# Loading the adjacency of a two-layer graph attention kernel through GpSimd's DMA queue, converted to bfloat16 on the way

## The chip, the cores and the metric

The kernel runs on one core of one Trainium2 chip. A core has a matrix engine (PE in the profile, with its weight loads listed as PEld), a vector engine (DVE), a scalar engine (ACT), GpSimd (POOL) and a sync engine (SP) that mostly issues transfers; 16 DMA engines move the data. The metric is the device time of one execution in microseconds (us). Every version has to give the outputs of the reference.

## The reference, cut to what matters

```python
# x: (8192, 128) float32; adj: (8192, 8192) int32 of zeros and ones, one in 1024 is a one
h = jnp.maximum(_layernorm(x), 0.0)
Whs, Wht, Whc = h @ Ws, h @ Wt, h @ Wc            # 64, 64 and 128 wide
z = jnp.where(adj > 0, Whs @ Wht.T, -9e15)
x = x + softmax(z, axis=-1) @ Whc                 # layer 0
h = jnp.maximum(_layernorm(x), 0.0)
Wh = h @ W
e = leaky_relu((Wh @ a1)[:, None] + (Wh @ a2)[None, :], 0.2)
x = x + elu(softmax(jnp.where(adj > 0, e, -9e15), axis=1) @ Wh)   # layer 1
```

The adjacency is 256 MB. Everything else is small: x is 4 MB.

## The kernel before

The 8192 queries are cut into 64 tiles of 128. For a tile, a key matters only if one of its 128 queries has an edge to it. The kernel therefore reads the adjacency of the tile (4 MB), finds the keys that are used, gathers at most 32 of every block of 128 keys with one-hot matrix products, and computes attention over these 2048 slots alone. The one-hot matrices and the gathered mask of each tile are stored to HBM (`sel_pick`, `sel`), and layer 1 works from them, so the adjacency is read only once, in layer 0. If a block had more than 32 used keys, a branch that works over all keys would be taken; with these inputs it is not.

The input `adjB` is laid out so that a tile is four chunks (c = 0 to 3) of 1 MB, in each of which a partition gets one contiguous row of 2048 int32 (16 key blocks of 128 queries). A chunk lands in `adj_st[:, c]`, of which there is one buffer for each c, named `arena` in the profile like most buffers here.

The stages of a run, by the profile's time: a preparation of about 75 us (layer norm of x in four quarters, transposes, projections), in which GpSimd's `make_h` (line 598) normalises two of every four rows of tiles; the tile sweep over 64 tiles up to about 940 us, which is a software pipeline that works on tile i's adjacency while it computes scores of tile i-2 and sums of tile i-4; a second preparation; and layer 1 from about 1000 us to the end.

In the sweep, step i (`tile_step`) holds on each engine, in program order:

- DVE: `convert` of chunks 0, 1 and 2 (line 1465: int32 to an fp8 mask, plus or minus one half), between them `maximum` (1512, 1515) and `make_pick` (1490, the one-hot matrices), then `indicate` (1472, which keys are used), `finish` (1529), and two `part_maximum` (1499) over the scores.
- ACT: evacuations from PSUM (1112, 1118, 1125), and among them `convert` of chunk 3 (line 1141), right ahead of the first of two `exps` (1132), which PE's first scores product of the next tile (764) waits for.
- PE: the gathers (725, 737, 752), the scores (763, 764, 769), the weighted sums (790).
- SP: `tile_io`. First the four `load_chunk` of the next tile, then the stores of the one-hot matrices (`store_pick`, line 454) and of the mask (`store_mask`, 448), 256 KB each, then one store of 64 KB (442) and one load of 64 KB (437).

`load_chunk(t, c)` waits until the previous tile's chunk in the same buffer has been converted (`conv_done` counts DVE's three, `conv_act` ACT's one) and then issues one transfer of 1 MB (line 434). SP is in order, so a chunk that waits for its buffer holds back what stands behind it: chunk 3 stands behind chunk 2, and the stores stand behind both. GpSimd does nothing in the sweep.

Of the kernel before, what the change touches and what calls it, by code (L numbers as in the profile page):

```python
# [11 lines left out]
BF16 = mybir.dt.bfloat16  # L12
F8 = mybir.dt.float8e4
I32 = mybir.dt.int32
# [4 lines left out]
P = 128  # L19
# [29 lines left out]
def gnn_kernel(nc, x, xB, adj, adjB, Ws, Wt, Wc, W1, a1, out, x_mid, sel, sel_pick):  # L49
    N = x.shape[0]  # L50
    TILES = N // P
# [10 lines left out]
    with ExitStack() as ctx:  # L62
# [6 lines left out]
        def sem(name):  # L69
            return ctx.enter_context(nc.semaphore(name))  # L70
# [3 lines left out]
        def part(start, words, dt=F32):  # L74
            view = arena[:, start:start + words]
            return view if dt == F32 else view.bitcast(dt)


        ADJ, VALS, KP, QQ, MASK, CC, POSX, VS, PT, K2, MS, END, TOP = (
            0, 8192, 16384, 20480, 28672, 32768, 34816, 36864, 40992, 43040, 44064, 45088, 46080)  # L80
        adj_st = part(ADJ, 8192, I32).rearrange("p (c b n) -> p c b n", c=4, n=P)
        c_vals = part(VALS, 8192, F16).rearrange("p (b v) -> p b v", v=2 * D)
        kp = part(KP, 4096, F16).rearrange("p (b k) -> p b k", k=2 * NHID)
        cq_hi = part(QQ, 4096, F16)
# [174 lines left out]
        adj_in = [sem(f"adj_in{c}") for c in range(4)]  # L259
        conv_done = sem("conv_done")  # L260
        conv_act = sem("conv_act")
# [71 lines left out]
        PREP = TILES // 4  # L333
# [4 lines left out]
        def wait(eng, s, value):  # L338
            if not (isinstance(value, int) and value <= 0):
                eng.wait_ge(s, value)  # L340

        def within(t, lo, hi):

            return not isinstance(t, int) or lo <= t < hi
# [12 lines left out]
        def there(i, d):  # L357

            return within(i, d, TILES + d)
# [36 lines left out]
        def by_choice(eng, selected_keys, all_keys):  # L396

            eng.wait_ge(decided, 1)
            ok = eng.value_load(edge_ok[0:1, 0:1], min_val=0, max_val=1)
            with eng.If(ok != 0):  # L400
                selected_keys()
            eng.wait_ge(decided_redo, 1)
            again = eng.value_load(redo[0:1, 0:1], min_val=0, max_val=1)
            with eng.If(again != 0):
                all_keys()
# [5 lines left out]
        def _(sp):  # L411
            def load_rows(src, mode, quarters=range(4)):
                n = TILES // 4
                for q in quarters:
                    rows = slice(q * n, (q + 1) * n)
                    sp.dma_start(x_all[mode][:, rows, :], src[:, rows, :]).then_inc(xall_in[q], 16)
# [7 lines left out]
                with nc.allow_non_contiguous_dma(reason="256 numbers"):  # L424
                    sp.dma_start(a_sb[:, :], a1.rearrange("(k d) o -> d (k o)", k=2)).then_inc(w_in, 16)

            def load_chunk(t, c):

                if c < 3:
                    wait(sp, conv_done, t * 3 + (c - 2))  # L430
                else:
                    wait(sp, conv_act, t)
                rows = adjB[bass.ds(t, 1), c, :, :, :].rearrange("o p b n -> p (o b) n")
                sp.dma_start(adj_st[:, c, :, :], rows).then_inc(adj_in[c], 16)  # L434

            def load_x(t, b):
                sp.dma_start(x_t[:, b, :], x[bass.ts(t, P), :]).then_inc(x_in[b], 16)

            def store_y(t, b):

                sp.wait_ge(y_ready, t + 1)
                sp.dma_start(x_midB[:, bass.ds(t, 1), :].rearrange("p o d -> p (o d)"), y_t[:, b, :]
                             ).then_inc(y_out[b], 16)

            def store_mask(t, b):

                sp.wait_ge(m_evac, t * 2 + 2)
                sp.dma_start(sel[bass.ds(t, 1), :, :].rearrange("o p n -> p (o n)"),
                             m_sel[:, b, :, :].rearrange("p s w -> p (s w)")).then_inc(m_out[b], 16)

            def store_pick(t, b):

                sp.wait_ge(pick_ready, t + 1)
                sp.dma_start(sel_pick[bass.ds(t, 1), :, :].rearrange("o p n -> p (o n)"), pick_w[:, b, :]
                             ).then_inc(pick_out[b], 16)

            def tile_io(i, b):
                if within(i, 0, TILES - 1):
                    for c in range(4):
                        load_chunk(i + 1, c)  # L460
                if there(i, 1):
                    store_pick(i - 1, 1 - b)
                if there(i, 2):
                    store_mask(i - 2, b)
                if there(i, 4):
                    store_y(i - 4, b)
                if within(i, 4, TILES + 2):
                    load_x(i - 2, b)
                if isinstance(i, int) and i == TILES:
                    sp.wait_ge(conv_done, TILES * 3)  # L470
                    sp.wait_ge(conv_act, TILES)
                    sp.wait_ge(y_out[0], 16 * (3 * TILES // 8))
                    sp.wait_ge(y_out[1], 16 * (3 * TILES // 8))
                    load_rows(x_midB, 1, range(3))
                if isinstance(i, int) and i == 4:
                    sp.wait_ge(mean_ready, 1)
                    sp.dma_start(w_sb[:, 0, :], W1).then_inc(w_in, 16)
# [1 line left out]
            load_rows(xB, 0, (0,))  # L479
            load_weights()  # L480
            load_rows(xB, 0, (1, 2, 3))
            for c in range(4):
                load_chunk(0, c)
            load_x(0, 0)
            load_x(1, 1)
            tile_sweep(sp, tile_io, fetched=False)
            sp.wait_ge(y_out[0], 16 * (TILES // 2))
            sp.wait_ge(y_out[1], 16 * (TILES // 2))
# [86 lines left out]
        @block.gpsimd  # L575
        def _(pool):
            nc.gpsimd.memset(ident[:, :], 0.0).then_inc(ident0, 1)
            pool.wait_ge(ident0, 1)
            nc.gpsimd.affine_select(out=ident[:, :], in_=ident[:, :], compare_op=ALU.not_equal, fill=1.0,
                                    base=0, pattern=[[-1, P]], channel_multiplier=1).then_inc(ident_ready, 1)  # L580
            nc.gpsimd.memset(tri_f[:, :], 1.0).then_inc(tri0, 1)
            pool.wait_ge(tri0, 1)
            nc.gpsimd.affine_select(out=tri_f[:, :], in_=tri_f[:, :], compare_op=ALU.is_ge, fill=0.0,
                                    base=0, pattern=[[1, P]], channel_multiplier=-1).then_inc(const_pool, 1)
            nc.gpsimd.iota(slot_i[:, :], pattern=[[1, SLOT]], base=1, channel_multiplier=0).then_inc(const_pool, 1)
            nc.gpsimd.memset(ones_b[:, :], 1.0).then_inc(const_pool, 1)
            nc.gpsimd.memset(bounds[:, :], 0.0).then_inc(const_pool, 1)

            def make_h(G, b, mode):

                tiles = range(G * NGRP + 2, G * NGRP + NGRP)
                for k, (lo, hi) in enumerate(SPANS[mode]):
                    if lo <= tiles[0] < hi:
                        pool.wait_ge(rstd_ready, BEFORE[mode] + k + 1)
                pool.wait_ge(xall_in[G // 4], 16 * (mode + 1))
                wait(pool, hT_ps_ready, mode * PREP + G - 1)
                for i, tile in enumerate(tiles):
                    last = nc.gpsimd.tensor_scalar(h_sb[mode][:, b, (2 + i) * P:(3 + i) * P], x_all[mode][:, tile, :],
                                                   rstd[:, 2, tile:tile + 1], rstd[:, 3, tile:tile + 1],
                                                   ALU.mult, ALU.add)  # L600
                last.then_inc(h_pool, 1)

            for mode in range(2):
                for G in range(PREP):
                    make_h(G, G % 2, mode)

            def mask(tau, m):

                pool.wait_ge(g_adj_in[m // 2], 16 * (tau + 1))
                wait(pool, masked, tau * STEPS + (m - 3))  # L610
                pool.sem_inc(pool_settled, 1)
                nc.gpsimd.tensor_scalar(off_sb[:, m % 4, :], adj_sb[:, m // 2, CW:2 * CW], 0.0, OFF,
                                        ALU.is_le, ALU.mult).then_inc(mask_pool, 1)

            def masks(layer):
                for m in range(1, STEPS, 2):
                    mask(layer * TILES, m)
                with pool.Fori(1, TILES) as t:
                    for m in range(1, STEPS, 2):
                        mask(t + layer * TILES, m)  # L620

            def all_keys():
                masks(0)
                masks(1)

            by_choice(pool, lambda: None, all_keys)
# [1365 lines left out]
```

## Time and profile before

| | |
|---|---|
| Runs | 1398.08, 1403.41 and 1406.76 us; median 1403.41 |
| Profiled execution, its own span | 1402.6 us |
| Busy in it: PE / DVE / ACT / POOL | 1276.6 / 1250.6 / 1024.8 / 32.3 us |
| HBM read / written | 319.03 / 41.94 MB |
| Adjacency loads | 256 of 1024 KB, median 7.3 us from issue to landing |

The profile is of one execution. A line names the source line, the engine, the operation, and what is written from what; a median or mean is per instruction. "[1.13 <-DMA ...]" behind an instruction says that its engine sat idle for 1.13 us and what ended that. The chain of waits follows the end of the work back, at each step to what released it. "DMA share" is the mean busy share of the 16 DMA engines.

### The profile page before, as it was taken

The numbers are of one execution on the slowest core, as the hardware profiler recorded it, in microseconds if no ns is written. First come the engines' busy times: TensorE is split into PE (matmuls) and PEld (weight loads), VectorE is DVE, ScalarE is ACT, GpSimd is POOL, SyncE is SP. The second block draws the span as 40 slices with busy tenths as digits, with TensorE's granted clock in tenths as the row PEclk, the third lists the DMA queues.
The fourth block names the chain that finished last, engine by engine and source line by source line (L and its number), as shares of the span: only waits on it lengthen the run. The fifth ranks groups of instructions, "written<-read, shape, count | busy, mean of one in ns | idle before, by whom it ended". The sixth has DMA issues, their size and how long they took to land.

```text
span 1402.6 us, 76097 instructions
## 1 busy us (share of the span) xinstructions
PE 1276.6 (91%) x31819; PEld 1131.9 (81%) x31947; DVE 1250.6 (89%) x2323; ACT 1024.8 (73%) x2036; POOL 32.3 (2%) x75
## 2 busy tenths in 40 slices
PE   5867899999999999999999999989899999999996
PEld 3656788888888888878878888877799999999995
DVE  8877799999999999989999999847899999999996
ACT  5755576767667677667676666748789999999994
POOL 2200000000000000000000000013000000000000
PEclk9979899999999999999999999999899999999998
DMA  6678899999999999999999999531134244334322
GB/s 249 248 266 287 280 345 369 370 381 368 368 391 357 377 378 366 383 380 341 382 378 361 376 374 374 223 114 55 56 108 121 81 124 123 108 94 123 117 85 72
DMA packets 104081, 363.10 MB, mean 259 GB/s; under 512 B 11520, under 2 KB 36352, under 8 KB 70144
## 3 DMA queue, kind: packets, MB, share of 16 engines
q1 hardware_dynamic: 103936, 361.02, 71.2%
q8 instruction: 109, 1.79, 0.5%
q14 instruction: 36, 0.29, 0.1%
HBM read 319.03 MB, written 41.94 MB: 257 GB/s over the span
## 4 chain that ended last, share of the span: by engine, by line
PE 46%; DMA 18%; DVE 16%; issue 12%; ACT 5%; SPq 1%; DVEq 1%; ACTq 0%; POOL 0%; POOLq 0%
DMA arena<-in_adjB 18%; PE ps L883 16%; PE ps L857 9%; DVE arena L1490 5%; PE ps L769 4%; DVE arena L1465 4%; PE ps L764 3%; PE ps L737 3%; DVE mx L1499 2%; ACT arena L1132 2%; PE ps L790 2%; PE ps L725 2%; PE ps L763 1%; PE ps L664 1%; SPq L434 1%
## 5 line engine op out<-in xcount | busy, mean ns | idle before, releaser
L790 PE MATMUL ps<-arena 128*128 128x129 f32 x2048 | 249.0, 280 | 0.4 <-issue 0.4
L1118 ACT ACTIVATE arena<-ps 128x512 f32<-128x512 f32 x256 | 153.2, 598 | 129.8 <-PE ps L737 129.8
L883 PE MATMUL ps<-arena 128*128 128x129 f32 x2048 | 245.1, 278 | 0.4 <-issue 0.4
L790 PEld LDWEIGHTS ps<-arena 128*128 128x128 f32 x2048 | 240.6, 196 | 0.6 <-issue 0.6
L1465 DVE TENSOR_SCALAR arena<-arena 128x2048 fp8e4<-128x2048 int32 x192 | 234.9, 1224 | 3.5 <-PE ps L752 1.5
L883 PEld LDWEIGHTS ps<-arena 128*128 128x128 f32 x2048 | 236.8, 194 | 0.5 <-issue 0.5
L1708 DVE TENSOR_SCALAR arena<-arena 128x128 f32<-128x128 f32 x768 | 202.4, 339 | 19.5 <-issue 14.3
L1112 ACT ACTIVATE arena<-ps 128x512 f16<-128x512 f32 x256 | 153.9, 601 | 52.5 <-PE ps L725 52.3
L769 PEld LDWEIGHTS ps<-arena 128*128 128x128 f16 x2048 | 137.5, 99 | 62.0 <-issue 2.2
L1499 DVE TENSOR_REDUCE mx<-ps 128x1 f32<-128x1024 f32 x128 | 155.7, 1216 | 29.9 <-PE ps L769 29.3
L737 PE MATMUL ps<-arena 128*32 128x128 f16 x8192 | 165.3, 223 | 16.5 <-issue 10.7
L1141 ACT ACTIVATE arena<-arena 128x2048 fp8e4<-128x2048 int32 x64 | 122.4, 1912 | 78.6 <-DMA arena<-in_adjB 78.5
L857 PE MATMUL ps<-arena 128*32 128x132 f16 x8192 | 153.2, 226 | 13.6 <-ACT arena L1178 4.5
L1178 ACT ACTIVATE arena<-ps 128x396 f32<-128x396 f32 (+1 forms) x384 | 148.2, 463 | 20.0 <-PE ps L857 19.9
L769 PE MATMUL ps<-arena 128*128 (+1 forms) x2048 | 158.1, 221 | 0.0
L857 PEld LDWEIGHTS ps<-arena 128*32 128x32 fp8e4 x8192 | 131.1, 98 | 32.0 <-issue 15.9
L1132 ACT ACTIVATE arena<-ps,neg_max 128x1024 f32<-128x1024 f32 x128 | 142.1, 1110 | 18.3 <-PE ps L790 18.2
L737 PEld LDWEIGHTS ps<-arena 128*32 128x32 fp8e4 x8192 | 121.6, 97 | 37.6 <-issue 21.4
L1717 DVE SCALAR_TENSOR_TENSOR arena<-arena 128x1024 f32<-128x1024 fp8e4 x128 | 150.6, 1215 | 0.5 <-ACT arena L1198 0.5
L1472 DVE TENSOR_REDUCE arena<-arena 128x64 f32<-128x2048 f32 x64 | 146.3, 2286 | 3.4 <-ACT arena L1141 0.8
L725 PE MATMUL ps<-arena 128*128 128x32 fp8e4 x4096 | 143.2, 177 | 4.1 <-DVE arena L1408 3.1
L1490 DVE TENSOR_TENSOR arena<-arena 128x2048 fp8e4<-128x2048 f16 x64 | 146.2, 2284 | 0.1
(165 smaller groups left out, 1400.4 us busy)
## 6 DMA issues: line engine op xcount, KB each, us to landing
arena<-in_adjB SPq DMA_DIRECT2D x256, 1024.0 KB, 7.3
sel_pick<-arena SPq DMA_DIRECT2D x64, 256.0 KB, 9.6
sel<-arena SPq DMA_DIRECT2D x64, 256.0 KB, 9.5
arena<-sel_pick SPq DMA_DIRECT2D x64, 256.0 KB, 3.8
arena<-sel SPq DMA_DIRECT2D x64, 256.0 KB, 2.8
arena<-in_xB SPq DMA_DIRECT2D x4, 1024.0 KB, 6.1
x_t<-in_x SPq DMA_DIRECT2D x64, 64.0 KB, 8.0
x_mid<-y_t SPq DMA_DIRECT2D x64, 64.0 KB, 8.3
```

Source lines behind the costliest of these rows:

```text
L725: last = nc.tensor.matmul(kg_ps[:, k * SLOT:(k + 1) * SLOT], kp[:, g * SB + k, :], pick[:, b, g * SB + k, :], start=True, stop=True)
L737: last = nc.tensor.matmul(vg_ps[j * SLOT:(j + 1) * SLOT, s * D:(s + 1) * D], pick[:, b, k, :], c_vals[:, k, l * D:(l + 1) * D], start=(l = ...
L769: last = nc.tensor.matmul(dst[:, k * P:(k + 1) * P], k_sel[:, at:at + P], rows[:, bass.ts(t, P)], start=False, stop=(n == 1), skip_group_c ...
L790: last = nc.tensor.matmul(pv_ps, p_T[:, s * P:(s + 1) * P], v_sel[:, b, s, :], start=False, stop=(s == SB - 1), skip_group_check=True)
L857: last = nc.tensor.matmul(xg_ps[g % 3][j * SLOT:(j + 1) * SLOT, at:at + XW], pick[:, b, s * QB + j, :], wv[:, s * QB + j, l, :], start=(l ...
L883: last = nc.tensor.matmul(xv_ps[b], w_msk[:, b, s, :], x1_sel[:, b, s, 0:VW], start=False, stop=(s == SB - 1), skip_group_check=True)
L1112: nc.scalar.activation(k_sel[:, g * GW:(g + 1) * GW], kg_ps, ACT.Copy).then_inc(k_evac, 1)
L1132: nc.scalar.activation(p_T[:, h * 1024:(h + 1) * 1024], ps[:, 2 * h:2 * h + 2, :].rearrange("p b n -> p (b n)"), ACT.Exp, bias=neg_max[:, ...
L1465: nc.vector.tensor_scalar(mask_8[:, b, c * QCH:(c + 1) * QCH, :], adj_st[:, c, :, :], 0.0, 0.5, ALU.is_gt, ALU.subtract, saturate=False).t ...
L1490: nc.vector.tensor_tensor(pick[:, b, :, :], posx.unsqueeze(2).to_broadcast(wide), slots[:, :].unsqueeze(1).to_broadcast(wide), ALU.is_equa ...
L1499: nc.vector.reduce_max(mx[:, h:h + 1], ps[:, 2 * h:2 * h + 2, :].rearrange("p b n -> p (b n)"), AX_X).then_inc(part_max, 1)
L1708: last = nc.vector.tensor_scalar(w_raw[b][:, k, :], own, x1_sel[:, b, k, D + 2:D + 3], x1_sel[:, b, k, D + 1:D + 2], ALU.mult, ALU.max)
```

## The change

All 256 loads of the adjacency move from SP's queue to GpSimd's. The source stays int32 and the destination becomes bfloat16, so the DMA converts on the way, and 512 KB instead of 1 MB are written into SBUF for each chunk. The two conversions to fp8 (lines 1465 and 1141) stay and read bfloat16 now. On GpSimd the loads of tile 0 come ahead of the first `make_h`, those of tile 1 between four of the `make_h` groups, those of tile 2 behind the last group of the first preparation, and the rest in a loop of their own; the second preparation's `make_h` comes behind that loop. SP keeps all other transfers.

```diff
-        adj_st = part(ADJ, 8192, I32).rearrange("p (c b n) -> p c b n", c=4, n=P)
+        adj_st = part(ADJ, 4096, BF16).rearrange("p (c b n) -> p c b n", c=4, n=P)
@@ sync engine
-            def load_chunk(t, c):
-                ...
-                sp.dma_start(adj_st[:, c, :, :], rows).then_inc(adj_in[c], 16)
             def tile_io(i, b):
-                if within(i, 0, TILES - 1):
-                    for c in range(4):
-                        load_chunk(i + 1, c)
                 if there(i, 1):
                     store_pick(i - 1, 1 - b)
                 ...
             load_rows(xB, 0, (1, 2, 3))
-            for c in range(4):
-                load_chunk(0, c)
@@ GpSimd
-            for mode in range(2):
-                for G in range(PREP):
-                    make_h(G, G % 2, mode)
+            def load_chunk(t, c):
+                if c < 3:
+                    wait(pool, conv_done, t * 3 + (c - 2))
+                else:
+                    wait(pool, conv_act, t)
+                rows = adjB[bass.ds(t, 1), c, :, :, :].rearrange("o p b n -> p (o b) n")
+                pool.dma_start(adj_st[:, c, :, :], rows).then_inc(adj_in[c], 16)
+            for c in range(4):
+                load_chunk(0, c)
+            for G in range(PREP):
+                make_h(G, G % 2, 0)
+                if 8 <= G < 12:
+                    load_chunk(1, G - 8)
+            for c in range(4):
+                load_chunk(2, c)
+            with pool.Fori(3, TILES) as t:
+                for c in range(4):
+                    load_chunk(t, c)
+            for G in range(PREP):
+                make_h(G, G % 2, 1)
```

## Rows read from the trace of the kernel before

**Rows 1.** The page: busy us of each engine, share of the span, instructions.
```profile
PE 1276.6 (91%) x31819; PEld 1131.9 (81%) x31947; DVE 1250.6 (89%) x2323; ACT 1024.8 (73%) x2036; POOL 32.3 (2%) x75
```
**Rows 2.** Stretches: length, busy (and instructions) by engine, PE clock, DMA share, GB/s.
```profile
188.00:884.00 696.00, 650.42 (x17514) 574.04 (x17610) 652.84 (x856) 484.24 (x694) 0.00 (x0) 1.00 0.99 372
486.37:512.39 26.02, 24.30 (x672) 21.47 (x668) 24.48 (x32) 18.09 (x27) 0.00 (x0) 1.00 1.01 381
```
**Rows 3.** DMA, 188 to 884 us: packets, MB, share; then issues, KB each, us to landing.
```profile
q1 hardware_dynamic: 61829, 259.11, 99.2%
...
arena<-in_adjB SPq DMA_DIRECT2D x215, 1024.0 KB, 7.3
sel_pick<-arena SPq DMA_DIRECT2D x53, 256.0 KB, 9.6
```
**Rows 4.** Line 434, 188 to 884 us: issue ns, first and last; who waited; landing.
```profile
L434 SPq DMA_DIRECT2D arena<-in_adjB x215: 328/333/355, 188.0 to 883.7; - x108
...
  ACT arena L1141: 74.4, 50
...
DMA to landing us min/median/max: 5.1/7.3/10.4
```
**Rows 5.** Waits, 300 to 800 us: total us, times, longest.
```profile
ACT arena L1141 <- DMA arena<-in_adjB: 52.4, 35, 2.8
...
DVE mx L1499 <- PE ps L769: 15.2, 30, 1.8
```
**Rows 6.** The chain of waits, 480 to 530 us: start, us, what.
```profile
480.82 9.37 DMA arena<-in_adjB
...
506.70 9.39 DMA arena<-in_adjB
```
**Rows 7.** Instructions of DVE in order of time, from 486 to 513 us.
```profile
486.37 1.23 DVE L1465 TENSOR_SCALAR arena<-arena 128x2048 fp8e4<-128x2048 int32 x1
...
498.17 1.22 DVE L1499 TENSOR_REDUCE mx<-ps 128x1 f32<-128x1024 f32 x1 [0.65 <-PE ps L769]
...
499.75 1.23 DVE L1465 TENSOR_SCALAR arena<-arena 128x2048 fp8e4<-128x2048 int32 x1
...
501.36 1.23 DVE L1465 TENSOR_SCALAR arena<-arena 128x2048 fp8e4<-128x2048 int32 x1
502.50 2.28 DVE L1490 TENSOR_TENSOR arena<-arena 128x2048 fp8e4<-128x2048 f16 x1
...
504.81 1.22 DVE L1465 TENSOR_SCALAR arena<-arena 128x2048 fp8e4<-128x2048 int32 x1
...
506.15 2.29 DVE L1472 TENSOR_REDUCE arena<-arena 128x64 f32<-128x2048 f32 x1
...
510.81 1.22 DVE L1499 TENSOR_REDUCE mx<-ps 128x1 f32<-128x1024 f32 x1 [0.16 <-PE ps L769]
...
512.39 1.23 DVE L1465 TENSOR_SCALAR arena<-arena 128x2048 fp8e4<-128x2048 int32 x1
```
**Rows 8.** Issues of SP in order of time, from 501 to 514 us.
```profile
501.15 5.89 SPq L434 DMA_DIRECT2D arena<-in_adjB  x4
507.22 0.36 SPq L454 DMA_DIRECT2D sel_pick<-arena  x1
507.76 0.35 SPq L448 DMA_DIRECT2D sel<-arena  x1
```
**Rows 9.** ACT's conversion of chunk 3 in the same tile.
```profile
503.02 1.91 ACT L1141 ACTIVATE arena<-arena 128x2048 fp8e4<-128x2048 int32 x1 [1.13 <-DMA arena<-in_adjB]
```
**Rows 10.** Instructions of GpSimd in order of time, in the first preparation.
```profile
11.94 1.74 POOL L598 TENSOR_SCALAR arena<-arena,rstd 128x128 f32<-128x128 f32 x4 [9.49 <-DVE rstd L1379]
...
39.50 1.27 POOL L598 TENSOR_SCALAR arena<-arena,rstd 128x128 f32<-128x128 f32 x2 [1.72 <-PE ps L641]
```
**Rows 11.** The chain of waits at the start: start, us, what.
```profile
0.82 5.06 DMA arena<-in_xB
```
**Rows 12.** DVE's first work on x.
```profile
5.90 3.19 DVE L1337 BATCH_NORM_STATS2 stat<-arena 128x6 f32<-128x128 f32 x16 [2.19 <-DMA arena<-in_xB]
```

More of the change, by code:

```diff
@@ L425, in load_weights @@
                     sp.dma_start(a_sb[:, :], a1.rearrange("(k d) o -> d (k o)", k=2)).then_inc(w_in, 16)
-            def load_chunk(t, c):
[L429 to L433, printed above, removed]
-                sp.dma_start(adj_st[:, c, :, :], rows).then_inc(adj_in[c], 16)
             def load_x(t, b):
```

## The prediction

> **What bounds the kernel now.** I read the page's busy times first. Three engines are near each other, PE, DVE and then ACT, and GpSimd is idle [rows 1], so no single engine settles it. The stage that holds the adjacency loads is the sweep, so I went on to a table of stretches: from 188 to 884 us the DMA share is 0.99 at 372 GB/s, PE is busy for 650 and DVE for 653 of 696 us [rows 2]. Line 434 issues 215 loads there, the first at 188.0 and the last at 883.7, which is 695.7 / (214 / 4) = 13.0 us a tile [rows 4], and 259.11 MB / 53.75 tiles = 4.82 MB a tile [rows 3]. At the 381 GB/s of the better stretch that is 12.65 us. So the DMA engines have almost no room.
>
> Who notices it? Over 500 us of the sweep ACT waits 35 times for a chunk of the adjacency, always chunk 3, for 52.4 us in all, while DVE's longest wait is for PE's scores, 15.2 us [rows 5]. The chain of waits shows how the two are joined: it runs through a load of chunk 3 of 9.37 us and then, 25.88 us later, through the next of 9.39 us [rows 6], that is once in two tiles. In DVE's order of time the two tiles of such a pair are 486.37 to 499.75 (13.38 us, 0.65 us of it waiting for scores) and 499.75 to 512.39 (12.64 us, 0.16 us waiting) [rows 7]. A late chunk 3 holds ACT (1.13 us in the tile shown, [rows 9]), ACT's late exponentials hold PE, and PE holds DVE. Without any wait the tile of DVE is 12.64 - 0.16 = 12.48 us. Two limits therefore lie within half a microsecond of each other: DVE's own work, 12.48, and the bytes, 12.65; the tile takes 13.0.
>
> **The change, part by part.**
>
> *DVE's and ACT's conversions.* They stay, 3 of 1.22 us on DVE and one of 1.91 us on ACT a tile [rows 7, 9]; only the source is 16 bit wide now. No row has a conversion from 16 bit to fp8 alone. The nearest is L1490, two f16 inputs to fp8, 2.28 us for 2048 elements, no faster than the float32 reduction L1472 over as many (2.29) [rows 7]; L1465 is already at about half of that. I take 0. The ends are 1.06 us more each (as slow as L1490) and, downwards, no more than the byte limit lets through, 13.0 - 12.65 = 0.35 us a tile, 53.5 x 0.35 = 19 us. The Trainium skill weighs against my 0: *VectorE: DVE Perf Modes*, "The perf-mode tier table", gives a bfloat16 `tensor_scalar` of 2048 elements 693 ns, where a 32-bit one takes 1227 ns; the trace agrees with the second number (1.22 us) and cannot show the first, and the page's conditions for its top mode ask for 16-bit tensors on both sides, which an fp8 output is not. By the 693 ns DVE would save 1.6 us a tile and DMA would be alone in front.
>
> *The bytes.* Read from HBM: the same 4 MB a tile. Written to SBUF: half. Since every chunk is still read at 4 bytes an element, I take the pace of 381 GB/s by bytes read, unchanged. No row shows a converting transfer. The ends: the pace of now, and one chunk at a time without any overlap, for which the start of the kernel gives 5.06 us for 1 MB alone [rows 11], 20.2 us a tile.
>
> *GpSimd's issue.* SP issues a load in 0.33 us [rows 4]. For GpSimd there is no row of an issue. The ends are 0.33 us and the length of one conversion, 1.22 us; I take 0.9 us, nearest to two of its own small operations (1.74 for four, so 0.87 for two [rows 10]). A longer issue by itself is hidden: chunks 2 and 3 are issued together behind the conversion that ends at 506.03 [rows 7] (the four issues end at 507.04 [rows 8]), while the queue still holds most of chunk 1. What is late next, if the cover went, is chunk 3 again, by up to 2 x 0.9 = 1.8 us.
>
> *What an issue does to DVE.* Chunk 0's buffer comes free at the end of the conversion that starts at 499.75, at 500.98, and the next conversion starts at 501.36, 0.38 us later [rows 7]. If an issue on GpSimd keeps a conversion on DVE from starting, that one is 0.9 - 0.38 = 0.5 us late. The other three issues lie beside L1490, and L1472 (2.28 and 2.29 us). Ends: 0 and 1.22 - 0.38 = 0.84 us a tile. I take 0.5 us. It counts in full where DVE sets the pace, one tile of two, and not in the other, where DVE waits 0.65 us for scores anyway: 0.25 us a tile, 53.5 x 0.25 = 13 us. The rule behind this is in the Trainium skill, *SBUF — State Buffer*, "Who interferes with whom": GpSimd and DVE share one pair of ports, which a `tensor_scalar` with both operands in SBUF takes for the whole instruction, and GpSimd needs it to write descriptors. No run so far shows it, since GpSimd is idle in the sweep.
>
> *The order of the transfers.* This is the part of the move that is easily missed. On SP the two stores of 256 KB stand behind chunks 2 and 3 and go out at 507.22 and 507.76, after chunk 3 [rows 8]. L1490, which they wait for, is done at 504.8 [rows 7]. With the loads gone from SP, the stores go at about 504.9 and 505.3, ahead of chunks 2 and 3. Their 512 KB and the two small transfers of 64 KB are 0.65 MB / 381 GB/s = 1.7 us of work for the DMA engines, of which up to 1.4 us (the two stores) comes before chunk 3, the one chunk that is already late. Nobody waits for the stores. Ends: 0 (the total of bytes is the same, and chunk 0 of the next tile comes earlier by as much) and 1.4 us a tile. Chunk 3 has no slack in 35 of some 38 tiles [rows 5], so I take 0.2 us, a seventh, because a load that is late in one tile leaves less to do in the next: 53.5 x 0.2 = 11 us.
>
> *GpSimd's other work.* `make_h` of G = 8 to 11 gets one issue each behind it; between its groups GpSimd waits 1.72 us for PE [rows 10], which hides 0.9 us. The waits of `load_chunk(1, c)` are for tile 0's conversions, and what they could hold up is `make_h` of the next group, which PE's transposes need; that is bounded by one conversion and one issue, 1.22 + 0.9 us, against the same 1.72 us, so 0.4 us at the worst. `make_h` of the second preparation is queued behind the loop and starts after it anyway. I take 0.
>
> *The start.* SP issued chunk 0 to 3 of tile 0 behind all of x. Now GpSimd issues them at about 2.3 us, while the first quarter of x is in flight (0.82 to 5.88 us [rows 11]), and DVE waits for that quarter already, 2.19 us [rows 12]. If the two share the engines evenly, the last 2.5 us of that transfer become up to 5 us. Ends 0 and 2.5 us; I take 2.
>
> *The first tiles of the sweep.* Of the 256 loads of the whole run 41 lie before 188 us [rows 4], that is ten tiles at over 14 us each even if they had begun at 40 us, longer than either limit; what is added per tile hides there, and I take 0.
>
> Sum: 13 + 11 + 2 = 26 us against the span of 1402.6 us, which is 0.8 us from the median of the runs: 1428 us, or 13.45 us a tile.
>
> **The rivals.**
>
> *Hidden (1390 to 1417).* The loads are limited by the read side, GpSimd's issues fall where DVE doesn't mind, the order evens out. For it: the total of bytes to read is the same, three of the four issues lie beside operations of 2.3 us. Against: the two limits are so close that nothing has cover. Time: 1403, with the 2 us of the start 1405.
>
> *The other side: chunk 3 comes earlier.* With half of the bytes to write, a DMA engine is sooner ready for the next row. It decides once a chunk lands 1.1 us earlier than now, which frees ACT. Then DVE's 12.48 us are the tile: 53.5 x (13.0 - 12.48) = 28 us, 1375 us; by half of that 1389. For it: the share of 0.99. Against: nothing says that writing is what takes the time.
>
> *The conversion slows the transfer.* Each tenth that the pace of the loads loses costs, since the loads are 4.19 of the 4.82 MB (11.0 us), 1.2 us a tile and over 61 tiles some 74 us. At three quarters of the pace: 14.7 + 1.7 = 16.4 us a tile, 1403 + 61 x 3.4 = 1610 us. At one chunk at a time, 20.2 us: 1403 + 61 x 7.2 = 1842 us. For it: the DMA engines have no room at all, so any loss shows one to one. Against: no row.
>
> **How the numbers follow.** Forecast (1417 to 1460, its own range 1410 to 1465) 0.32; hidden 0.26; earlier 0.16; slower conversion 0.26, of which 0.16 above 1620. The range leaves out that 0.16 and 0.04 below 1388, so it is 1388 to 1620. A measurement of this kernel can tell about 1% from no change (its three runs lie within 0.6%). Faster by over 1% is the earlier-chunk rival, 0.16; within 1% is hidden and the lower edge of the forecast, 0.30; slower is the rest, 0.54.
>
> **What would show it.** In the table of stretches: about 372 GB/s read by the loads and a tile of 13.2 to 13.6 us; by the slower-conversion rival a DMA share still near 1 but a lower pace, loads landing after more than 12 us, and DVE waiting for DMA. DVE: L1465 still 1.22 us, and an idle of about 0.5 us ahead of chunk 1's that is put down to nothing in the profile. SP: the stores issued right after L1490, before chunk 2. ACT: L1141's wait for chunk 3 longer than 52 us in 500. DVE's first work on x at 7 to 8 us instead of 5.9. The prediction is wrong if GpSimd takes over 2 us an issue, or if the conversion costs the DMA engines time.

## The result, and the profile after

The changed kernel takes 1455.18 us (median, 1444.83 to 1459.55) where the kernel before takes 1403.99. The ratio is 1.0347, with a 95% interval of 1.0296 to 1.0398: 51 us slower. The forecast was 1428 us. The direction was right, the size was half of what came.

The page of the kernel after: busy times first ([rows 1] of before), then the two DMA queues, then three groups of instructions (busy us, mean ns of one, and the engine's idle time ahead of them with what ended it):

```profile
PE 1278.6 (88%) x31819; PEld 1131.0 (78%) x31947; DVE 1254.6 (87%) x2323; ACT 1025.8 (71%) x2036; POOL 200.2 (14%) x331
...
q0 software_dynamic: 36864, 134.23, 50.8%
q1 hardware_dynamic: 67072, 92.56, 20.4%
...
L596 POOL DMA_DIRECT2D arena<-in_adjB x256 | 168.8, 660 | 705.5 <-DVE arena L1470 632.0
...
L1470 DVE TENSOR_SCALAR arena<-arena 128x2048 fp8e4<-128x2048 bf16 x192 | 234.9, 1224 | 3.0 <-PE ps L757 1.0
...
L1146 ACT ACTIVATE arena<-arena 128x2048 fp8e4<-128x2048 bf16 x64 | 122.3, 1912 | 119.6 <-DMA arena<-in_adjB 119.5
```

PE, DVE and ACT do the same work in the same busy time as before, within 4 us. What grew is idle time: ACT's wait for chunk 3 is 119.5 us in the whole run, where the page of before has 78.5:

```profile
L1141 ACT ACTIVATE arena<-arena 128x2048 fp8e4<-128x2048 int32 x64 | 122.4, 1912 | 78.6 <-DMA arena<-in_adjB 78.5
```

GB/s and MB after are counted by the bytes written, so a chunk counts 512 KB.

The same stretch as [rows 2], the issues as in [rows 4], and the waits as in [rows 5], all of the kernel after:

```profile
188.00:884.00 696.00, 618.55 (x16676) 544.37 (x16775) 620.65 (x812) 457.55 (x657) 135.74 (x201) 0.99 0.98 201
```
```profile
L596 POOL DMA_DIRECT2D arena<-in_adjB x201: 527/528/1115, 193.5 to 882.7; - x101
...
  ACT arena L1146: 103.4, 48
...
DMA to landing us min/median/max: 5.5/8.0/11.1
```
```profile
ACT arena L1146 <- DMA arena<-in_adjB: 75.6, 35, 4.0
...
PE ps L769 <- ACT arena L1137: 49.3, 25, 3.2
...
DVE mx L1504 <- PE ps L774: 22.8, 42, 1.8
DVE arena L1477 <- ACT arena L1146: 16.3, 19, 1.5
```

A tile takes (882.7 - 193.5) / (200 / 4) = 13.78 us instead of 13.0. DMA share is 0.98, hardly less than before. A load takes 8.0 us to land instead of 7.3, and ACT waits for chunk 3 for 75.6 instead of 52.4 us in 500.

The chain of waits from 480 to 540 us, its conversions, loads and GpSimd's last piece ahead of a load ([rows 6] of before):

```profile
499.52 1.15 DVE arena L1470
...
501.31 0.06 POOL arena L596
...
501.86 11.12 DMA arena<-in_adjB
...
527.69 1.15 DVE arena L1470
...
529.47 0.06 POOL arena L596
...
530.02 10.62 DMA arena<-in_adjB
```

It still passes through chunk 3 once in two tiles. It comes to that load from DVE's third conversion of the tile (line 1470), through GpSimd's queue, where chunk 3 stands behind chunk 2.

One tile in order of time (DVE, ACT, POOL and SP; [rows 7] to [rows 9] are the same place before):

```profile
501.29 1.10 POOL L596 DMA_DIRECT2D arena<-in_adjB  x2 [2.91 <-ACT arena L1146]
...
508.40 1.23 DVE L1470 TENSOR_SCALAR arena<-arena 128x2048 fp8e4<-128x2048 bf16 x1
...
510.02 1.23 DVE L1470 TENSOR_SCALAR arena<-arena 128x2048 fp8e4<-128x2048 bf16 x1
510.25 1.11 POOL L596 DMA_DIRECT2D arena<-in_adjB  x1 [7.86 <-DVE arena L1470]
...
511.87 0.53 POOL L596 DMA_DIRECT2D arena<-in_adjB  x1 [0.51 <-issue]
513.17 1.91 ACT L1146 ACTIVATE arena<-arena 128x2048 fp8e4<-128x2048 bf16 x1 [2.63 <-DMA arena<-in_adjB]
...
513.47 1.22 DVE L1470 TENSOR_SCALAR arena<-arena 128x2048 fp8e4<-128x2048 bf16 x1
513.63 0.33 SPq L445 DMA_DIRECT2D sel_pick<-arena  x1
...
514.25 0.33 SPq L439 DMA_DIRECT2D sel<-arena  x1
...
515.31 1.10 POOL L596 DMA_DIRECT2D arena<-in_adjB  x2 [2.91 <-ACT arena L1146]
```

Three things stand in it. The conversion of chunk 0 ends at 509.63, and GpSimd's issue starts 0.62 us later and is done at 511.36, 1.73 us behind the end; on SP it was 0.50 us ([rows 8]: 501.15 + 0.33, behind 500.98). The stores go out at 513.63 and 514.25, ahead of chunks 2 and 3. And chunk 3 lands late for ACT. Its issue ends at 502.39, it lands at about 513.0, ACT converts it until 515.08, and its next issue ends at 516.41.

Two things can hold that next issue: ACT, which frees chunk 3's one buffer, and chunk 2 ahead of it in the queue, which DVE's third conversion frees (at 514.69 here). In this tile they are almost even. Over 48 tiles (12 to 59), chunk 3's buffer had been free for 1.25 us in the median when its issue started, and the issue followed ACT's conversion directly (within 0.75 us) in 21 of them; before, for 1.48 us, and in 4. So in more than half of the tiles it is the place behind chunk 2 that holds it. The "ACT" in the brackets of the issue at 515.31 is the profile's guess: the first of its two issues starts 0.62 us behind DVE's conversion and only 0.23 behind ACT's.

DVE's conversion at 510.02 starts 1.62 us behind the one ahead of it, as before (1.61), and over the 48 tiles the mean is 1.62 us in both kernels: GpSimd's issue beside it costs DVE nothing.

At the start, DVE's first work on each of the first two quarters of x:

```profile
6.06 3.19 DVE L1342 BATCH_NORM_STATS2 stat<-arena 128x6 f32<-128x128 f32 x16 [2.21 <-DMA arena<-in_xB]
20.75 3.19 DVE L1342 BATCH_NORM_STATS2 stat<-arena 128x6 f32<-128x128 f32 x16 [8.75 <-DMA arena<-in_xB]
```

The first quarter comes 0.16 us later than in [rows 12], the second after a wait of 8.75 us that the kernel before did not have.

### The profile page after: what moved, and what is told of

Its sections match the earlier page's. It is cut to its first block, busy times and chain, and to the rows that moved or that the text cites. A ratio compares the mean times of both kernels' runs of the same rounds, so it can differ in the third digit from the quotient of the medians.

```text
span 1449.5 us, 76328 instructions
## 1 busy us (share of the span) xinstructions
PE 1278.6 (88%) x31819; PEld 1131.0 (78%) x31947; DVE 1254.6 (87%) x2323; ACT 1025.8 (71%) x2036; POOL 200.2 (14%) x331
## 3 DMA queue, kind: packets, MB, share of 16 engines
q8 instruction: 108, 1.77, 0.5%
## 4 chain that ended last, share of the span: by engine, by line
PE 43%; DMA 22%; DVE 15%; issue 14%; ACT 5%; DVEq 1%; POOL 0%; ACTq 0%; SPq 0%; POOLq 0%
DMA arena<-in_adjB 21%; PE ps L888 16%; PE ps L862 9%; DVE arena L1495 4%; PE ps L774 4%; DVE arena L1470 4%; PE ps L769 3%; DVE mx L1504 2%; ACT arena L1137 2%; PE ps L742 2%; PE ps L795 1%; PE ps L730 1%; PE ps L768 1%; DMA arena<-in_xB 1%; PE ps L669 1%
## 5 line engine op out<-in xcount | busy, mean ns | idle before, releaser
L596 POOL DMA_DIRECT2D arena<-in_adjB x256 | 168.8, 660 | 705.5 <-DVE arena L1470 632.0
L1470 DVE TENSOR_SCALAR arena<-arena 128x2048 fp8e4<-128x2048 bf16 x192 | 234.9, 1224 | 3.0 <-PE ps L757 1.0
L1146 ACT ACTIVATE arena<-arena 128x2048 fp8e4<-128x2048 bf16 x64 | 122.3, 1912 | 119.6 <-DMA arena<-in_adjB 119.5
L769 PE MATMUL ps<-arena 128*128 128x512 fp8e4 x256 | 98.9, 386 | 86.6 <-ACT arena L1137 75.5
## 6 DMA issues: line engine op xcount, KB each, us to landing
arena<-in_xB SPq DMA_DIRECT2D x4, 1024.0 KB, 17.5
```

Of the source, the lines that this page charges most:

```text
L596: pool.dma_start(adj_st[:, c, :, :], rows).then_inc(adj_in[c], 16)
L1470: nc.vector.tensor_scalar(mask_8[:, b, c * QCH:(c + 1) * QCH, :], adj_st[:, c, :, :], 0.0, 0.5, ALU.is_gt, ALU.subtract, saturate=False).t ...
```

## The experiments

Ratios are to the kernel before, on the same chip, with 95% intervals. "A tile" is here the time from the issue of chunk 0 of tile 12 to that of tile 60, divided by 48. The 13.00 and 13.78 us of above come from a window that ends at different chunks of a tile; over the 48 whole tiles they are 13.02 and 13.76.

| | median us | ratio | us a tile |
|---|---|---|---|
| before | 1403.5 | 1 | 13.02 |
| after | 1455.2 | 1.035 (1.030 to 1.040) | 13.76 |
| e1_pool_int32 | 1454.2 | 1.038 (1.033 to 1.043) | 13.77 |
| e2_stores_first | 1424.9 | 1.015 (1.012 to 1.019) | 13.46 |
| e3_stores_last | 1458.9 | 1.041 (1.037 to 1.045) | 13.79 |
| e4_sp_swap | 1372.1 | 0.978 (0.975 to 0.982) | 12.48 |
| e5_start | 1442.3 | 1.029 (1.026 to 1.031) | 13.77 |
| e6_pool_swap | 1386.7 | 0.987 (0.984 to 0.990) | 12.69 |
| e7_double | 1375.7 | 0.979 (0.977 to 0.982) | 12.42 |
| e8_sp_late | 1429.1 | 1.021 (1.015 to 1.027) | 13.54 |
| e9_sp_both | 1434.1 | 1.021 (1.019 to 1.024) | 13.59 |
| e10_double_start | 1367.6 | 0.974 (0.971 to 0.976) | 12.42 |

**The conversion undone** (e1_pool_int32, on the kernel after)

```diff
-        adj_st = part(ADJ, 4096, BF16).rearrange(...)
+        adj_st = part(ADJ, 8192, I32).rearrange(...)
```

> The changed kernel with one thing undone: the chunks stay int32 (1 MB into SBUF), and GpSimd still issues them. If the converting transfer itself is what got slower (a row of a chunk took 2.88 us of all 16 engines for a chunk after, 2.72 before), most of the time of the sweep comes back: about 1415 us, the rest being the later start of 9.6 us. If GpSimd's queue is what costs (later issues, the order against the stores), nothing comes back: 1450 to 1460 us.

1454.2 us and 13.77 us a tile: nothing comes back. The converting transfer is not what costs; what came with the loads to GpSimd's queue is. The stretch and the queues of it show that the engines had room:

```profile
188.00:884.00 696.00, 633.30 (x16716) 544.42 (x16717) 621.88 (x807) 457.39 (x657) 134.78 (x201) 0.99 0.94 351
```
```profile
q0 software_dynamic: 28994, 211.19, 80.4%
q1 hardware_dynamic: 29084, 33.29, 13.2%
```

The DMA share is 0.94 instead of 0.98 and the tile is as long. So the share of 0.98 after was not a limit.

**Loads alone** (m1_pace: none of the computation). In each stretch, four buffers, and each is loaded again as soon as it has landed:

```diff
+ STRETCHES = [("sp", "i32", False), ("pool", "i32", False), ("pool", "bf16", False),
+              ("sp", "i32", True), ("pool", "i32", True), ("pool", "bf16", True)]
```

"True" is a stretch with the two stores of 256 KB for each tile.

> Loads alone: none of the computation, the output is a copy of x. Six stretches of 10 tiles (40 chunks) each, a chunk's next load issued as soon as its last has landed: by SP as int32, by GpSimd as int32, by GpSimd as bfloat16, and then the same three with the two stores of 256 KB for each tile from SP. If the conversion slows the engines by the 6% of the rows in the changed kernel, the third stretch takes 6% longer than the first (about 11.0 us a tile, 11.7 for the converted). If the queue does it, the second does too. If neither, all three take 11.0 us a tile, and with stores 12.5.

One window inside each stretch, in that order (columns: length, busy DVE, busy POOL, PE clock, DMA share, GB/s):

```profile
10.00:100.00 90.00, 0.00 (x0) 0.00 (x0) 1.00 1.01 422
110.00:200.00 90.00, 0.00 (x0) 18.92 (x36) 1.00 1.01 422
214.00:296.00 82.00, 0.00 (x0) 17.40 (x33) 1.00 1.06 213
320.00:410.00 90.00, 0.00 (x0) 0.00 (x0) 1.00 1.01 422
440.00:530.00 90.00, 0.00 (x0) 16.89 (x32) 1.00 1.02 424
560.00:640.00 80.00, 0.00 (x0) 14.77 (x28) 1.00 1.06 233
```

Neither the queue nor the conversion slows a stream: 422 GB/s from SP and from GpSimd, and 213 written, which is 426 read, with the conversion. By the spacing of the stores a tile of four loads and two stores takes 11.21 us on SP (344.31 to 355.52 us; two of the nine took 11.8 and 11.9), 11.1 on GpSimd and 11.25 converted. I had expected 12.5 with stores and 11.0 without; without, 4.19 MB at 422 GB/s are 9.9. The 12.65 us that I had called the byte limit, from 381 GB/s, were no limit: the engines can do 422 when four loads are always under way.

**Who holds whom** (m2_lock: loads alone, with a busy DVE)

```diff
+ STRETCHES = [("pool", "bf16", None), ("pool", "bf16", "copy"), ("pool", "bf16", "max"),
+              ("sp", "i32", None), ("sp", "i32", "copy"), ("sp", "i32", "max")]
```

With "None" DVE is idle, with "copy" it does 96 conversions back to back, with "max" 52 maxima.

> Loads alone and a busy DVE: none of the computation, the output is a copy of x. Six stretches of 10 tiles: GpSimd's converting loads with DVE idle, with DVE in back-to-back conversions of 2048 elements from bfloat16 to fp8, and with DVE in back-to-back maxima over 2048 elements; then the same three with SP's int32 loads. If a conversion on DVE keeps GpSimd from issuing, the issue of 0.53 us takes up to 1.7 us in the second stretch and 0.53 in the third, and SP's issues (0.33 us) are alike in all three. If the 1.1 us issues of the changed kernel have another cause, the first three are alike too. If DVE's conversions are held up by GpSimd, some of them last longer than 1.22 us.

GpSimd's issues, one of the first stretch, three of the second, the first four of the third (one row) and a later one:

```profile
87.77 0.53 POOL L46 DMA_DIRECT2D buf_b<-in_adjB  x1 [1.89 <-DMA buf_b<-in_adjB]
...
163.65 1.56 POOL L46 DMA_DIRECT2D buf_b<-in_adjB  x1 [1.85 <-DMA buf_b<-in_adjB]
166.11 1.37 POOL L46 DMA_DIRECT2D buf_b<-in_adjB  x1 [0.90 <-DMA buf_b<-in_adjB]
168.60 1.15 POOL L46 DMA_DIRECT2D buf_b<-in_adjB  x1 [1.12 <-DMA buf_b<-in_adjB]
...
205.70 7.73 POOL L46 DMA_DIRECT2D buf_b<-in_adjB  x4 [8.62 <-DMA buf_b<-in_adjB]
...
241.12 0.53 POOL L46 DMA_DIRECT2D buf_b<-in_adjB  x1 [1.93 <-DMA buf_b<-in_adjB]
```

DVE's 96 conversions beside GpSimd's loads, then beside SP's:

```profile
102.37 109.36 DVE L74 TENSOR_SCALAR m<-src 128x2048 fp8e4<-128x2048 bf16 x96 [98.17 <-SPq L58]
...
414.29 109.08 DVE L74 TENSOR_SCALAR m<-src 128x2048 fp8e4<-128x2048 bf16 x96 [88.51 <-SPq L58]
```

An issue that meets a conversion takes up to 1.56 us instead of 0.53 in the second stretch; one that meets a maximum takes 0.53. The row at 205.70 holds one that is far longer: DVE was still at its conversions, which ran until 211.73, and the first of the four issues took 6.14 us and ended at 211.84, 0.11 us behind the last of them. Why that one waited through several conversions and the 40 of the second stretch did not, no run shows. DVE loses 0.28 us in 96 conversions. So in these runs DVE holds GpSimd and is not held, and that is the direction that I had not priced. An issue that is under way before DVE's conversion begins was not set up.

**The order of the transfers** (e2_stores_first, on the kernel before)

```diff
-                    for c in range(4):
+                    for c in range(2):
                         load_chunk(i + 1, c)
                 ... store_pick, store_mask
+                    for c in range(2, 4):
+                        load_chunk(i + 1, c)
```

> The kernel before, with SP's issue order changed to chunk 0, chunk 1, the two stores of 256 KB, chunk 2, chunk 3, as it comes about in the changed kernel. If the order of the transfers costs, 1404 becomes 1415 to 1440 us. If it does not, 1404 within 0.5%.

21 us slower, 0.44 us a tile, with nothing moved to another engine and nothing converted. But it is not the order in the DMA engines alone. SP's issues of the loads, ns at the least, in the median and at the most (before: 328/333/355, [rows 4]):

```profile
L434 SPq DMA_DIRECT2D arena<-in_adjB x206: 332/354/1792, 189.0 to 876.6; - x103
```

The long ones are those behind the two stores: over 48 tiles chunk 2's issue takes 0.53 us in the mean and chunk 3's 0.84, instead of 0.33 each. So chunk 3's ends 1.77 us behind DVE's third conversion, where it was 1.01 before, and its flight grew by only 0.12 us (9.18 instead of 9.06). Why SP's issues take longer there, no run shows.

**Each issue later** (e8_sp_late, on the kernel before; IDLE = 14)

```diff
+                for _ in range(IDLE):
+                    sp.sem_inc(idled, 1)
                 sp.dma_start(adj_st[:, c, :, :], rows).then_inc(adj_in[c], 16)
```

> The kernel before, with 14 semaphore increments of SP ahead of each load, which hold each issue back by about 0.6 us, as GpSimd does (1.15 us from the end of a conversion to the end of the issue behind it, against 0.5 us on SP). If the lateness of the issues is the larger part of the loss: 1425 to 1440 us. If it is hidden by the loads in flight: 1404 us within 0.5%.

27 us slower. It holds more than GpSimd does: the end of chunk 3's issue comes 2.70 us behind DVE's third conversion (503.53 + 1.22, then SP's four issues from 500.84 for 6.61 us), against 1.72 us after and 1.0 before. So it shows that lateness is not hidden, at about 0.3 us a tile for each 1 us, and not how much of it is GpSimd's.

**Both, in GpSimd's size, on SP** (e9_sp_both: e2's order, and IDLE = 6)

> The kernel before with the two habits of the changed one put on SP, without GpSimd and without the conversion: the two stores of 256 KB ahead of chunks 2 and 3, and 6 semaphore increments ahead of each load, which bring the end of chunk 3's issue from 1.0 to about 1.7 us behind DVE's third conversion, as on GpSimd. If these two together are the loss of the sweep (13.00 to 13.78 us a tile), a tile takes 13.6 to 13.9 us and the run 1435 to 1445 us. If something else of GpSimd's queue is needed for it, the run stays at the 1425 us of the stores alone.

1434.1 us and 13.59 us a tile, both at the lower edge of what was expected, with chunk 3's issue done 1.8 us behind the third conversion in the median. Of the 0.74 us that a tile lost, 0.57 appear on SP with these two habits alone, and 31 of the 51 us.

The traces say where the rest is. From the end of DVE's third conversion to the landing of chunk 3, means over the 48 tiles, in us:

| | to the end of its issue | its flight | both | a tile |
|---|---|---|---|---|
| before | 1.01 | 9.06 | 10.07 | 13.02 |
| e2_stores_first | 1.77 | 9.18 | 10.95 | 13.46 |
| e8_sp_late | 2.77 | 8.18 | 10.95 | 13.54 |
| e9_sp_both | 1.94 | 9.23 | 11.17 | 13.59 |
| after | 1.97 | 9.52 | 11.49 | 13.76 |
| e1_pool_int32 | 1.87 | 9.72 | 11.59 | 13.77 |
| e3_stores_last | 1.82 | 9.79 | 11.61 | 13.79 |

In all six the tile grew by 0.5 to 0.6 of what the landing came later, about what a path taken once in two tiles gives. e9 has the lateness of the issue whole; what it lacks is 0.29 us of flight. That the flight is longer from GpSimd's queue, converted or not, these rows show; why, no run shows. Chunk 0's issue, which GpSimd ends 1.73 us behind its conversion and e9 about 0.9, is another difference, and it was not tried alone.

**The start** (e5_start, on the kernel after)

```diff
-            for c in range(4):
-                load_chunk(0, c)
             for G in range(PREP):
                 make_h(G, G % 2, 0)
+                if G == 1:
+                    pool.wait_ge(xall_in[3], 16)
+                    for c in range(4):
+                        load_chunk(0, c)
```

> The changed kernel, with GpSimd's loads of tile 0 behind the second group of make_h and the landing of all of x, so that they no longer share the DMA engines with x. DVE starts on the second quarter of x at 20.75 us after, where before its first conversion came 9.6 us sooner. If that start is worth its full length: 1445 us, 9 to 10 us less than the changed kernel. If it is hidden by the first tiles of the sweep: 1454 us.

1442.3 us, 13 us less than the kernel after by the medians and 10.7 by the profiled executions. DVE starts on the second quarter of x at 11.83 us again, and on its first conversion at 35.7 instead of 44.1 (34.4 before). The same mend on top of two buffers (e10_double_start against e7_double, below) gives 8 us. So the start is worth 8 to 13 us, about its length, and the first tiles of the sweep do not hide it.

**The stores held back** (e3_stores_last, on the kernel after: GpSimd counts its issues of chunk 3, and SP waits for that count ahead of the stores)

```diff
+                if c == 3 and not (isinstance(t, int) and t < 2):
+                    pool.sem_inc(adj_issued, 1)
@@ SP, tile_io
+                if within(i, 1, TILES - 1):
+                    sp.wait_ge(adj_issued, i)
```

> The changed kernel, and SP waits until GpSimd has issued chunk 3 of the next tile before it issues the two stores of 256 KB, which is the order of before. If the stores ahead of chunk 3 are what makes it later, ACT's wait for chunk 3 falls back and some 30 of the 51 us are gone: 1420 to 1430 us. If the pace of the transfer or the delay of GpSimd's issues counts, nothing: 1450 to 1460 us.

No gain. The expectation was missed, and the timeline says that the order was only half restored:

```profile
504.98 1.10 POOL L599 DMA_DIRECT2D arena<-in_adjB  x2 [2.91 <-ACT arena L1151]
505.72 0.33 SPq L446 DMA_DIRECT2D sel_pick<-arena  x1
506.24 0.33 SPq L440 DMA_DIRECT2D sel<-arena  x1
```

The count goes up while GpSimd still works on the issue, so the first store goes out at 505.72, before chunk 3's issue ends at 506.08, and on another queue. Chunk 3's flight did not get shorter (9.79 us, against 9.52 in the kernel after). What the run shows is that this wait does not buy the order back; why the flight stays long is open.

**Chunk 3 first** (e4_sp_swap on the kernel before, e6_pool_swap on the kernel after)

```diff
-                    for c in range(4):
+                    for c in (0, 1, 3, 2):
                         load_chunk(i + 1, c)
```

> The kernel before, with chunk 3 issued ahead of chunk 2, since ACT frees chunk 3's buffer about 1.1 us before DVE frees chunk 2's. If the lateness of chunk 3 is what binds the kernel before beyond DVE's own work, it is faster: 13.0 us a tile become 12.6 to 12.8, 1380 to 1395 us. If the engines' pace alone binds, no change: 1404 us.

> The changed kernel, with chunk 3 issued ahead of chunk 2 on GpSimd in the sweep. If the loop of chunk 3's one buffer (issue, landing, ACT's conversion, issue) sets the 13.85 us of a tile, a sooner issue takes 0.5 to 1 us out of it: 1405 to 1425 us. If the pace of the engines sets it, no change: 1454 us.

Both came out better than expected (1372.1 against 1380 to 1395, 1386.7 against 1405 to 1425). On SP the swap is worth 31 us, on GpSimd 69 us, more than the change had cost. ACT's wait for chunk 3 in 500 us falls from 75.6 us to

```profile
ACT arena L1146 <- DMA arena<-in_adjB: 14.8, 22, 2.6
```

on GpSimd, although a load takes 9.1 us to land there, longer than 8.0. Chunk 3 no longer stands behind chunk 2: on GpSimd its issue now follows ACT's conversion directly in 47 of the 48 tiles, and ends 1.23 us ahead of DVE's third conversion instead of 1.97 behind it.

**Two buffers for each chunk** (e7_double, and with the start mended e10_double_start, on the kernel after)

```diff
-        adj_st = part(ADJ, 4096, BF16).rearrange("p (c b n) -> p c b n", c=4, n=P)
+        adj_st = part(ADJ, 8192, BF16).rearrange("p (u c b n) -> p u c b n", u=2, c=4, n=P)
-                    wait(pool, conv_done, t * 3 + (c - 2))
+                    wait(pool, conv_done, t * 3 + (c - 5))
-                    wait(pool, conv_act, t)
+                    wait(pool, conv_act, t - 1)
```

> The changed kernel, with two buffers for each chunk in the space that the half-size chunks leave free, so that a late issue or landing costs nothing as long as the DMA engines keep up. If the loop of the buffers (late issues, late landings) sets the time, a tile falls to what the engines need, about 13.5 us busy after or 13.0 by the unconverted loads: 1415 to 1435 us. If the converting transfer's pace sets it, the gain is under 0.3 us a tile: 1440 to 1455 us.

> Converting loads with two buffers for each chunk, and tile 0's loads behind x's. If the gain of the one (1376 us) and of the other (12 us) are independent, 1362 to 1368 us, which is below the kernel before and below chunk 3 ahead of chunk 2 on SP (1372 us). If the sweep swallows the start, 1374 us.

The chunks of half size leave as much room free as they take, and a second set of buffers takes them out of every loop. The stretch from 188 to 884 us of e7_double:

```profile
188.00:884.00 696.00, 692.03 (x18541) 597.45 (x18540) 675.66 (x896) 516.52 (x728) 144.21 (x215) 1.00 1.02 216
```

A tile takes 12.42 us, no engine waits for a chunk any more, and PE is busy for 692 and DVE for 676 of 696 us. I had expected 1415 to 1435 us, because I took 13.0 to 13.5 us a tile for what the DMA engines need; 1375.7 us shows that they need less. With the start mended it is 1367.6 us, 36 us below the kernel before, with stores first, late issues and conversion all in place.

## Why the prediction came out at half

**What bounds the kernel.** Half right. The path through chunk 3, once in two tiles ([rows 5, 6]), was the bound, and without it a tile takes about DVE's 12.48 us: 12.48 in e4, 12.42 in e7. In e7 PE is busier than DVE (692 and 676 of 696 us), so which of them is the floor stays open. The other limit, 12.65 us by the bytes, was wrong. I had read a DMA share of 0.99 at 372 GB/s as engines without room [rows 2]. A share says that something is under way, not that it goes at its best pace: e4 has the same 0.99 from 188 to 884 us at 381 GB/s, and alone the same loads go at 422 with 1.01.

**The conversions on DVE and ACT.** Right: 1224 and 1912 ns, unchanged with a 16-bit source. The 693 ns that the Trainium skill gives in *VectorE: DVE Perf Modes* for bfloat16 do not hold for an fp8 output, as the conditions on the page let one expect.

**The bytes.** Right: conversion costs no pace (m1_pace, e1_pool_int32). The rival with 0.26 on it, a slower transfer, is refuted. So is the one with 0.16, a chunk 3 that comes earlier: it came 1.43 us later (the table under e9).

**GpSimd's issue.** This is the step that failed. I wrote that a longer issue by itself is hidden, behind what the queue still holds, and put it at nothing. It is not hidden. The issue is shorter than the 0.9 us that I took, 0.53 us, but it starts 0.62 us behind the conversion that frees the buffer, where SP starts after 0.17, so that behind DVE's third conversion chunk 3 is handed over 0.72 us later in most tiles and 0.96 in the mean (the rest comes from tiles in which ACT freed the buffer last). ACT already waited for chunk 3 in 35 of some 38 tiles ([rows 5]), so what I had named as late next, if the cover went, had no cover to begin with. The issue's lateness is 0.96 of the 1.43 us by which chunk 3 lands later. By that share it is two thirds of the 38 us that the sweep lost, an estimate of 25 us. e8 shows on SP, without GpSimd, that such lateness costs. The rival that I called hidden, 1405 us, is out with this step.

**What an issue does to DVE.** Wrong: 13 us taken, nothing seen (1.62 us from one conversion to the next in both kernels). A conversion on DVE holds GpSimd's issue, to 1.1 us for chunk 0 in each tile, and the issue does not hold DVE. The rule of the Trainium skill in *SBUF — State Buffer*, "Who interferes with whom", says that whoever is first blocks the other; the runs agree with it for GpSimd behind DVE and show nothing of the reverse.

**The order of the transfers.** Counted as 11 us of bytes ahead of chunk 3 in the DMA engines. On SP the order alone costs 21 us (e2), but by another way than mine: 0.76 of the 0.88 us by which chunk 3 lands later are a later issue, 0.12 are flight. In the kernel after the stores go out on a queue of their own, and chunk 3's flight is 0.46 us longer than before, a third of the sweep's loss, some 13 us by the same estimate. That is near my 11, but e3, which holds the stores back until about chunk 3's issue, did not shorten the flight. So the cause of that third stays open, and the nearness of the numbers is luck.

**The start.** Right in kind, 2 us taken, 8 to 13 measured (e5, e10). I priced only the first quarter of x, which was nearly landed when GpSimd began. The next three quarters met 4 MB of loads from another queue, where on one queue they had been ahead of them: x's quarters land after 17.5 us in the median instead of 6.1.

The sum was 13 + 11 + 2 = 26. Measured, by the medians: 13 of start, and 38 for 0.74 us a tile, of which the two habits on SP reproduce 31. Half of the forecast was a cost that never came; without it the forecast would have been 13 us, a quarter of what was measured. The total came as near as it did by luck.

## What to carry to other kernels

Look for the load that the chain of waits runs through, and at what its issue stands behind. Here each microsecond that it landed later cost half a microsecond a tile. The cheapest mends were to issue that load ahead of one that lands with room to spare (chunk 2, which before had landed 4.6 us ahead of its conversion in the median), or to give it a second buffer. A DMA share near 1 does not show that the engines are at their pace: compare GB/s with a stream that always has several loads in flight. A queue that is split in two loses its order, and both what used to be behind and what used to be ahead has to be priced.

## What the runs showed of the hardware that I had not expected

- A load that converts int32 to bfloat16 goes at 426 GB/s by the bytes read, the plain one at 422. The DMA share of the converting stream is counted as 1.06.
- GpSimd issues a load of 128 rows in 0.53 us, converting or not, and beside DVE's back-to-back `tensor_scalar`s of 1.22 us in 0.53 to 1.56 us, once in 6.14 us (m2_lock); beside a reduction it stays at 0.53 us. DVE's conversions took 109.36 us for 96 beside it and 109.08 without it.
- Issued right behind two stores of 256 KB on the same queue (e2), SP's loads took 0.53 and 0.84 us to issue in the mean, and up to 1.79; before, 0.33.
- From the end of DVE's conversion to the start of the issue that waits for it passed 0.62 us on GpSimd and 0.17 us on SP.
